# Channel attention of one block formed from the Gram matrix of the normalised rows, with the softmax, value and output weights merged into one 128x128 matrix

## The reference, cut to what matters

```python
def A(x):                       # x: layernorm of the input; 8 heads of 16 channels
    xn = x * rsqrt(mean(x * x) + 1e-6) * norm_weight
    q, k, v = split(xn @ w_qkv.T)               # 512 x 128 each, heads on the channels
    q = l2norm(q over the 512 rows) * exp(temperature)
    k = l2norm(k over the 512 rows)
    sim = q.T @ k               # per head 16 x 16: channels attend to channels
    attn = softmax(sim)
    return (attn @ v.T).T @ w_out.T
x = x + A(layernorm(x)); x = x + F(layernorm(x)); x = x + B(layernorm(x)); x = x + F(layernorm(x))
```

## Time and profile before

| | |
|---|---|
| median of 3 runs | 577.84 us |
| their range | 575.66 to 580.05 us |
| profiled execution, span from the first to the last instruction | 573.3 us |
| its mean granted TensorE clock | 0.961 |
| busy PE / DVE / ACT / POOL | 499.5 / 496.8 / 342.9 / 333.1 us |

### The profile page before, as it was taken

One profiled execution on the slowest core, in us unless ns is written; L12 is line 12 of the kernel. 1 busy time (PEld: TensorE's weight loads), 2 busy tenths in 40 slices (PEclk: granted clock), 3 DMA queues, 4 the chain that ended last, 5 costly groups with the idle time before them and its releaser, 6 DMA issues.

```text
span 573.3 us, 7484 instructions
## 1 busy us (share of the span) xinstructions
PE 499.5 (87%) x2224; PEld 384.0 (67%) x2224; DVE 496.8 (87%) x938; ACT 342.9 (60%) x581; POOL 333.1 (58%) x275
## 2 busy tenths in 40 slices
PE   3678899999989779998779997779997999999996
PEld 2455677788757657776557775666775777677883
DVE  3557999697899999999997999988999779798875
ACT  3454774767646678557566557565584655745563
POOL 4324778765745556754655455563465647677673
PEclk9789998999989998999888999989997999999999
DMA  8400000000000000000000000000000000000000
GB/s 269 144 2 1 1 1 1 0 2 0 1 0 2 1 0 1 2 0 1 2 0 1 0 2 1 0 1 1 2 18 1 1 1 19 1 1 2 18 2 18
DMA packets 7780, 7.44 MB, mean 13 GB/s; under 512 B 700, under 2 KB 7612, under 8 KB 7740
## 3 DMA queue, kind: packets, MB, share of 16 engines
q1 hardware_dynamic: 7740, 6.97, 3.8%
HBM read 5.91 MB, written 1.05 MB: 12 GB/s over the span
## 4 chain that ended last, share of the span: by engine, by line
PE 46%; DVE 38%; issue 9%; ACT 4%; POOL 2%; DMA 1%; SPq 0%; DVEq 0%; ACTq 0%; POOLq 0%
PE bank L890 12%; PE bank L892 11%; PE bank L891 11%; DVE alo L834 8%; DVE t L827 6%; DVE xn L699 4%; PE bank L1062 2%; DVE mk L860 2%; DVE bst L685 2%; DVE mk L855 2%; DVE mk L851 1%; DVE bmx L864 1%; ACT ah L600 1%; PE bank L984 1%; PE bank L1053 1%
## 5 line engine op out<-in xcount | busy, mean ns | idle before, releaser
L497 POOL TENSOR_TENSOR t<-t,sl 128x512 f32<-128x512 f32 x168 | 261.7, 1568 | 176.7 <-DVE t L827 165.2
L834 DVE TENSOR_TENSOR alo<-t,ah 128x512 fp32r<-128x512 f32 x168 | 160.5, 955 | 33.3 <-ACT ah L600 32.7
L594 ACT ACTIVATE sl<-bank 128x512 f32<-128x512 f32 x168 | 100.4, 598 | 91.2 <-POOL t L497 72.6
L600 ACT ACTIVATE ah<-t 128x512 fp32r<-128x512 f32 x168 | 105.7, 629 | 68.2 <-PE bank L892 67.6
L827 DVE TENSOR_TENSOR t<-bank,sbc 128x512 f32<-128x512 f32 x168 | 113.9, 678 | 3.9 <-PE bank L892 3.9
L890 PE MATMUL bank<-xhF,WUh 128*128 128x512 f32 x168 | 71.2, 424 | 24.1 <-DVE t L827 24.0
L890 PE MATMUL bank<-xhF,WGh 128*128 128x512 f32 x168 | 76.8, 457 | 0.1
L890 PE MATMUL bank<-ah,WDh 128*128 128x512 f32 x168 | 69.0, 411 | 4.3 <-DVE alo L834 2.4
L892 PE MATMUL bank<-xhF,WUl 128*128 128x512 f32 x168 | 68.4, 407 | 0.0
L892 PE MATMUL bank<-xhF,WGl 128*128 128x512 f32 x168 | 68.2, 406 | 0.0
L891 PE MATMUL bank<-xlF,WUh 128*128 128x512 f32 x168 | 68.2, 406 | 0.0
(11 more groups left out here) (168 smaller groups left out, 800.5 us busy)
## 6 DMA issues: line engine op xcount, KB each, us to landing
stage<-in_gate SPq DMA_DIRECT2D x7, 192.0 KB, 6.2
stage<-in_up SPq DMA_DIRECT2D x7, 192.0 KB, 6.3
stage<-in_down SPq DMA_DIRECT2D x7, 192.0 KB, 6.2
X<-in_x SPq DMA_DIRECT2D x4, 256.0 KB, 5.6
out<-X SPq DMA_DIRECT2D x4, 256.0 KB, 2.3
raw<-in_small SPq DMA_DIRECT2D x1, 580.0 KB
rows<-in_row SPq DMA_DIRECT2D x1, 136.0 KB, 5.8
cols<-in_columns SPq DMA_DIRECT2D x1, 3.0 KB
```

Of the source, the lines that this page charges most:

```text
L497: pool.tensor_tensor(t2[k % NT2][:, :], t2[k % NT2][:, :], sl[k % NSL][:, :], ALU.mult).then_inc(a_done, 1)
L594: act.activation(sl[k % NSL][:, :], bank[k % 2][:, :], ACT.Silu).then_inc(silu_done, 1)
L600: act.activation(ah[k % 2][:, :], t2[k % NT2][:, :], ACT.Copy).then_inc(ahi_done, 1)
L834: dve.tensor_tensor(alo[k % 2][:, :], t2[k % NT2][:, :], ah[k % 2][:, :].bitcast(F32), ALU.subtract).then_inc(alo_done, 1)
```

## The change

Batch by batch, A is computed in another order. `ag` multiplies the normalised rows with themselves, xn.T xn, a 128x128 Gram matrix, straight from `xn`; `ar` multiplies it by the q and k weights (128x256); `asim` gets k.T q from one product with the k weights, and the sums of squares from the weights times that product (`qsq`, made by DVE) summed over the channels. Behind the softmax, `am` multiplies its transpose by the output weights, which DVE has scaled by the reciprocal row sums (`wo`), `am2` multiplies by the value weights (transposed once, `wv`), and `y` applies the resulting 128x128 matrix to the transposed rows. `aqk`, `av`, `aT` and `aav` are gone. The due times are shorter (a batch takes 17 instead of 21), the first two starts are nearer to chunk 0, and the costs that `plan()` counts with are those of the new steps. `xT` of a batch now needs `y` of the batch before, since the transposed rows are read last.

```diff
-A_STEPS = [(0, "stats"), (1, "xn"), (3, "xT"), (5, "aqk", 0), (6, "aqk", 1), (8, "av"), (10, "asim"),
-           (10, "ass"), (12, "ascale"), (14, "asT"), (14, "amax"), (15, "aexp"), (17, "aT"),
-           (19, "aav"), (21, "y")]
+A_STEPS = [(0, "stats"), (1, "xn"), (3, "ag"), (3, "xT"), (5, "ar"), (7, "asim"), (7, "ass"), (9, "ascale"),
+           (10, "asT"), (10, "amax"), (11, "aexp"), (13, "am"), (15, "am2"), (17, "y")]
-A_STARTS = (-42, -26, 1, 21)
+A_STARTS = (-38, -24, 1, 21)
...
-        return [("av", prev)]
+        return [("y", prev), ("ag", b)]
+    if kind == "am2" and b == 0:
+        return [("wv", 0)]
...
+    threads += [[A_STARTS[0] + 4, [(0, ("wv", 0))], 0]]
...
+                if kind == "ag":
...
+                    act.activation(gram[:, :], m_bank(t)[:, 0:P], ACT.Copy).then_inc(n_free(t), 1)
+                if kind == "ar":
...
+                    act.activation(gw[:, :, :].rearrange("p r c -> p (r c)"), m_bank(t)[:, 0:2 * P], ACT.Copy).then_inc(gw_ready, 1)
...
+                if kind == "am":
...
+                    act.activation(mix[:, :], m_bank(t)[:, 0:P], ACT.Copy).then_inc(n_free(t), 1)
+                if kind == "am2":
...
+                    act.activation(mixw[:, :], m_bank(t)[:, 0:P], ACT.Copy).then_inc(n_free(t), 1)
...
+                if kind == "ar":
...
+                    dve.wait_ge(gw_ready, b + 1)
+                    dve.tensor_tensor(qsq[:, :, :].rearrange("p r c -> p (r c)"), m_bank(t)[:, 0:2 * P],
+                                      raw[:, C_QKV:C_QKV + 2 * P], ALU.mult).then_inc(n_free(t), 1)
...
-                if kind == "aT":
+                if kind == "am":
                     b = s[1]
                     dve.wait_ge(aexp_done, b + 1)
...
                     dve.reciprocal(ari[:, :], ars[:, :]).then_inc(ari_ready, 1)
+                    dve.wait_ge(ari_ready, b + 1)
+                    dve.tensor_scalar(wo[:, :], raw[:, C_OUT:C_OUT + P], ari[:, 0:1], None, ALU.mult).then_inc(wo_ready, 1)
...
+                if kind == "wv":
...
+                    pe.transpose(turn(t)[:, 0:P], raw[:, C_QKV + 256:C_QKV + 384], ident[:, :]).then_inc(m_full[t % 3], 1)
+                if kind == "ag":
...
+                    for i in range(NT):
+                        r = pe.matmul(m[:, 0:P], xn[:, i, :], xn[:, i, :], start=(i == 0), stop=(i == NT - 1))
...
+                if kind == "ar":
...
+                    wait_free(pe, turn_of["ag", b])
+                    pe.matmul(turn(t)[:, 0:2 * P], gram[:, :], raw[:, C_QKV:C_QKV + 2 * P], start=True, stop=True)\
+                      .then_inc(m_full[t % 3], 1)
+                if kind == "asim":
...
+                    wait_free(pe, turn_of["ar", b])
+                    pe.matmul(m[:, 0:P], raw[:, C_QKV + P:C_QKV + 2 * P], gw[:, 0, :], start=True, stop=True)
+                    for j in range(2):
+                        r = pe.matmul(m[:, P + j:P + j + 1], qsq[:, 1 - j, :], ones[:, :], start=True, stop=True)
...
+                if kind == "am":
...
+                    pe.matmul(turn(t)[:, 0:P], attn[:, :], wo[:, :], start=True, stop=True).then_inc(m_full[t % 3], 1)
+                if kind == "am2":
...
+                    pe.matmul(turn(t)[:, 0:P], wvT[:, :], mix[:, :], start=True, stop=True).then_inc(m_full[t % 3], 1)
                 if kind == "y":
...
-                        r = pe.matmul(m[:, a], oA[:, a], raw[:, C_OUT:C_OUT + P], start=True, stop=True)
+                        r = pe.matmul(m[:, a], xaT[:, a], mixw[:, :], start=True, stop=True)
```

More of the change, by code:

```diff
@@ L93 @@
 F_AHEAD = 22
-TURNS = dict(xT=1, aqk=1, av=1, asim=1, asT=1, aT=1, aav=1, y=1, route=2, act=1, sbc=1, yT=1,
+TURNS = dict(xT=1, wv=1, ag=1, ar=1, asim=1, asT=1, am=1, am2=1, y=1, route=2, act=1, sbc=1, yT=1,
              bqk=1, bv=1, bs=1, bpT=1, bo=1, by=1)
 FREED_BY = dict(asim="ascale", asT="amax", act="actk", by="byx")
-COST = dict(stats=(0, 0, 1.2), xn=(0, 0, 1.1), xT=(.4, .5, 0), xl=(0, 0, .6), aqk=(.9, 1, 0), av=(.9, .5, 0),
-            asim=(1.3, 0, 0), ass=(0, 0, .1), ascale=(0, 0, .3), asT=(.1, 0, 0), amax=(0, 0, .5), aexp=(0, 3, 0),
-            aT=(.1, .2, .1), aav=(.9, .5, 0), y=(.9, 0, .6), route=(2, 1.1, .3), rexp=(0, 2.7, 0),
+COST = dict(stats=(0, 0, 1.2), xn=(0, 0, 1.1), xT=(.4, .5, 0), xl=(0, 0, .6), ag=(.9, .3, 0), ar=(.5, .4, .4),
+            asim=(.7, 0, 0), ass=(0, 0, .1), ascale=(0, 0, .3), asT=(.1, 0, 0), amax=(0, 0, .5), aexp=(0, 3, 0),
+            am=(.3, .3, .5), am2=(.3, .3, 0), y=(.9, 0, .6), route=(2, 1.1, .3), rexp=(0, 2.7, 0),
             rsum=(0, 0, 1.3), rrank=(0, 0, 1.1), tanh=(0, .5, 0), gelu=(0, 0, .6), act=(.9, 0, 0), actk=(0, 0, 1.3),
@@ L136, in needs @@
         return [("bo", prev, NT - 1)] + [("bexp", b, i) for i in range(NT)]
-    return {"aqk": [("asim", prev)], "av": [("aav", prev)], "ass": [("ascale", prev)],
-            "ascale": [("asT", prev), ("amax", prev)], "amax": [("aexp", prev)], "aexp": [("aT", prev)],
-            "aT": [("aav", prev)], "aav": [("y", prev)],
+    return {"ag": [("ar", prev)], "ar": [("asim", prev)], "ass": [("ascale", prev)],
+            "ascale": [("asT", prev), ("amax", prev)], "amax": [("aexp", prev)], "aexp": [("am", prev)],
+            "am": [("am2", prev)], "am2": [("y", prev)],
             "bqk": [("bs", prev, NT - 1)], "bs": [("bpT", prev, NT - 1)], "bv": [("bo", prev, NT - 1)],
@@ L524, in _ @@
                     act.activation(dst[:, :], m_bank(t)[:, :], ACT.Copy).then_inc(xh_ready, 1)
-                if kind == "aqk":
-                    _, b, j = s
+                if kind == "wv":
+                    t = turn_of[s]
+                    wait_full(act, t)
+                    act.activation(wvT[:, :], m_bank(t)[:, 0:P], ACT.Copy).then_inc(n_free(t), 1)
+                if kind == "ag":
+                    b = s[1]
+                    t = turn_of[s]
+                    if b:
+                        wait_full(act, turn_of["ar", b - 1])
+                    wait_full(act, t)
+                    act.activation(gram[:, :], m_bank(t)[:, 0:P], ACT.Copy).then_inc(n_free(t), 1)
+                if kind == "ar":
+                    b = s[1]
                     t = turn_of[s]
@@ L946, in _ @@
                     pe.wait_ge(aexp_done, b + 1)
-                    pe.transpose(turn(t)[:, 0:P], attn[:, :], ident[:, :]).then_inc(m_full[t % 3], 1)
-                if kind == "aav":
+                    pe.wait_ge(wo_ready, b + 1)
+                    pe.matmul(turn(t)[:, 0:P], attn[:, :], wo[:, :], start=True, stop=True).then_inc(m_full[t % 3], 1)
+                if kind == "am2":
                     b = s[1]
                     t = turn_of[s]
-                    wait_free(pe, turn_of["aT", b])
-                    pe.matmul(turn(t)[:, :], attnT[:, :], vT[:, :], start=True, stop=True).then_inc(m_full[t % 3], 1)
+                    if b == 0:
+                        wait_free(pe, turn_of["wv", 0])
+                    wait_free(pe, turn_of["am", b])
+                    pe.matmul(turn(t)[:, 0:P], wvT[:, :], mix[:, :], start=True, stop=True).then_inc(m_full[t % 3], 1)
                 if kind == "y":
@@ L955, in _ @@
                     t = turn_of[s]
-                    wait_free(pe, turn_of["aav", b])
+                    wait_free(pe, turn_of["am2", b])
+                    wait_free(pe, turn_of["xT", "A", b])
                     m = turn(t)
```

73 lines of the change are left out of this document (27 added, 46 removed).

## The result

The changed kernel takes 589.62 us in the median of 4 runs (588.66 to 592.25) against 577.85 before: a ratio of 1.020, 95% interval 1.0153 to 1.0247. It is slower by some 12 us, where 569 was predicted and everything over 577 was outside the range. The profiled execution has a span of 587.1 us and a time of 588.9; so 1.8 us lie around a span, not the 4.5 that the prediction took from another execution's median.

What follows compares the result with a forecast made beforehand. It took chain length ahead of chunk 0, then TensorE and DVE, as the bounds; gains of 3.2 + 2.5 + 2.2 + 1.0 = 8.9 us gave a span of 564.4, with 4.5 more 569 us, range 562.5 to 577.

Steps and rivals of the forecast that it cites:

- Waits that are added: Among the chunks: DVE's wait for gw costs 0.4 us; am's wait for aexp and xT's for y cost nothing.
- What bounds the kernel: Chain length ahead of chunk 0; TensorE and DVE at 90% from 50 to 113, TensorE to 150, DVE to 179.
- Only the head gains: Rival: DVE sets the pace from chunk 0, freed TensorE time turns into waits; 573.6 us, chance 0.23.
- The clock: Rival: less matmul work keeps TensorE's clock low; head gains 1.5, chunks nothing; 576 us, chance 0.10.
- DVE turns the sign: Rival: in batches 2 and 3 DVE's added work and waits lose 5.5 us each; 585.6 us, chance 0.07.
- Ahead of chunk 0: Before chunk 0: shorter chain and fewer waits in F's head, less two new delays, gain 3.2 us (1.5 to 5.5).
- all matmuls of the head at half clock: Lower bound of the gain before chunk 0: 1.5 us if those matmuls run at half clock.
- DVE's price: Per batch, qsq 0.45, wo 0.35 and an estimated 0.1 for the reciprocal: 0.9 us more on DVE, up to 1.9.
- TensorE's saving: 3.7 us less matmul work a batch; booked among the chunks as 2.5 for batch 2 and 2.2 for batch 3.
- The earlier F: F of batch 2 starts at chunk 20, not 24, moving DVE steps to TensorE-bound chunks: 1.0 us gained (0 to 3).

Runs made afterwards that it cites:

- fix2b: Changed kernel, in batches 2 and 3 wo its own step two chunks ahead of am, and asT, amax, aexp one chunk later; 574.98 us, ratio 0.9972.
- fix2c: Changed kernel, in batches 2 and 3 wo its own step two chunks ahead of am, and batch 3's ag and xT one chunk later; 577.08 us, ratio 0.9977.
- fix1: Changed kernel with a 20-chunk list in batches 2 and 3: wo its own step two chunks ahead of am, asT two behind ascale; 570.89 us, ratio 0.9911.
- e7: fix1 with five extra products of weights ahead of the waits of asT 0, am 0 and am 1, before chunk 0; 571.19 us, ratio 0.9893.
- e6: fix1 without qsq, its wait, and wo with its reciprocal in batches 2 and 3; 572.05 us, ratio 0.9928.
- e5b: Changed kernel with 16 and 22 extra matmuls ahead of am's waits in batches 2 and 3; 586.21 us, ratio 1.0136.
- e2: Changed kernel, but in batches 2 and 3 asT reads weights and doesn't wait there for DVE's ascale; 588.24 us, ratio 1.0201.
- fix1s: fix1 with one thing put back: wo in the same chunk as am in batches 2 and 3; 580.01 us, ratio 1.0029.

## Why the prediction was wrong, step by step

**The step that failed** is "Waits that are added". It priced DVE's wait for `gw` at 0.4 us, which came out at 0.2 in batch 2 and nothing in batch 3. Of the waits that TensorE got it looked at two and put both at nothing. Of `am` it said that its wait for `aexp` "is due two chunks behind it, so among the chunks nothing". That holds for `aexp`. But `am` on TensorE also waits for `wo`, and `wo` was put into the same step, so it stands in DVE's queue behind all that DVE still owes up to that chunk. TensorE came to `am` with chunk 15 done while DVE had yet to begin its scaling of chunk 15; the wait was 4.66 us there and 6.4 at chunk 35, and the two cost 8 to 10 us of time. `asT` was not named at all, though its due time moved from two chunks behind `ascale` to one: 7.5 us of waits, some 4 us of time (fix2b). Of `xT` the step said "nothing", looking at `y`; it was the bank, which F's `xl` frees, that it waited 2.4 us for: again some 4 us of time in the traces and 3 by the medians (fix2c). By the traces the three come to about what lies between the changed kernel and fix1: 10.2, 3.9 and 4.0, some 18 us, against 16.8 (18.9 by e7). For am three runs show it; for the other two the size is less certain.

**What bounds the kernel** was read rightly but thought of as a property of an engine. With both engines at 90%, an instruction at the head of TensorE's queue that needed DVE's latest work stopped both: TensorE for the wait (4.66 us at chunk 15), then DVE for what TensorE had not made (3.47).

**The rivals.** "Only the head gains" and "The clock" gave times under that of before. "DVE turns the sign" had the sign but not the place: it let DVE wait for ACT's `gw` and `am` for `aexp`, and not `am` for `wo`; leaving DVE's work out (e6) gains nothing. Its 585.6 us came nearest to the 589.62 measured, by terms that the trace doesn't show. The clock was low behind the waits, as a consequence of them, for some 3 of their 9 to 10 us (e5b).

**Ahead of chunk 0** the prediction had 3.2 us (1.5 to 5.5); the profiled execution shows 1.9, and other executions of the same list from nothing to 2.2, against one of the kernel before. The chain of A came out as worked: L764's successor ends at 25.84, where 25.5 was written. The rest of the timeline, changed kernel, and last the end of the same matmuls before:

```profile
25.16 0.68 DVE L779 TENSOR_TENSOR X<-bank,X 128x512 f32<-128x512 f32 x1
...
31.94 0.35 PE L992 MATMUL bank<-router,xhF 128*128 128x16 f32 x1 [0.90 <-issue]
...
34.64 0.63 PE L907 MATMUL bank<-xhF,SWl 128*128 128x512 f32 x1
...
40.69 0.68 DVE L814 SCALAR_TENSOR_TENSOR hq<-hq,xa 50x512 f32<-50x512 f32 x1
```
```profile
37.32 0.40 PE L892 MATMUL bank<-xhF,SWl 128*128 128x512 f32 x1
```

At the start of route the lead is 3.9 us (31.94 against 35.87); at gelu it is 2.1 (40.69 against 42.82). Route's matmuls took 3.3 us from the first to the end of L907 where they had taken 1.9 before: the granted clock was 0.58 from 31 to 36, and 0.97 from 35 to 38 before. That is the term that the prediction bounded by "all matmuls of the head at half clock", 1.5, which came out nearer than the value taken. Why the clock was low there is open: TensorE worked 0.5 of 5 us from 15 to 20, where it had worked 2.6 before, but in e7, where it worked 2.9, the clock in F's head was low too.

**DVE's price** (0.9 a batch) was that ahead of chunk 0, where wo took 0.29; in batches 2 and 3 wo took 1.09 and 1.10, so some 1.7 a batch, near the upper end of 1.9. It was as good as free where nobody waited for it (e6). **TensorE's saving** is real: fix1 has it and gains 5 us by the ratio, of which ahead of chunk 0 1.7 in its trace; it has 6.1 us of lead at chunk 42, here,

```profile
172.89 0.68 DVE L843 TENSOR_TENSOR t<-bank,sbc 128x512 f32<-128x512 f32 x1
```

and 3.0 at chunk 63. From chunk 11 to 63 it is 0.9 us faster than before, and e7 with the same list 3.0; the ratio leaves 3.4 for all chunks. The 4.7 us that were booked for TensorE's saving in batches 2 and 3 were thus too much by a quarter at least, even in a list without the waits. **The earlier F**, booked with 1.0 us, can't be seen as a gain: fix2b, which has it, isn't faster than fix1, and in the changed kernel it put `actk` ahead of `wo`.

## What to carry to other kernels

When a step is cut into a list that several in-order engines walk, look for each product in it at the engine that makes it and at the one that needs it, and count how far apart they stand in the two queues, not how long they take: an operation of 1.1 us in the same chunk as its reader cost 8 to 10 us over two batches here, and nothing that shows two chunks ahead of it. Where two engines were both near full, a saving in work was worth less than the distance between maker and reader. And a wait taken away may in part pass on to the next wait on the same queue, as asT's did to am's in e2; its price showed only once am's wait was gone.

## What was not expected of the hardware

TensorE's granted clock was low behind both waits of `am`, 0.69 and 0.54 over the 11 us around them, after TensorE had stood still for 4.66 and 6.44 us; with products put into the two waits (3.89 us of them in the first) it stayed at 1.00. The two instructions of `am`, an fp32 product of 128x128, took 0.77 us behind the empty wait and 0.46 behind the filled one.

`wo`, 0.29 us ahead of chunk 0, took 1.09 and 1.10 in the chunks, and both times it ended 0.08 us behind an operation of POOL that was running when it started: L497 until 98.94 and `wo` until 99.02, L480 until 169.42 and `wo` until 169.50. In e5b and fix1s the `wo` of batch 2 again took 1.09 and ended 0.08 us behind POOL's L497 or L498.
